# A mixing stage with half of its products on ScalarE and TensorE, the branch product first, and norms a tile earlier

## The reference, cut to what matters

```python
x_norm = x * rsqrt(mean(x * x) + RMS_EPS)
H_res_logits = x_norm @ W_res.T + H_res_base      # 4 x 4 per token
H_pre, H_post = softmax(...), softmax(...)        # 4 each per token
H_res = (1 - g) * I + g * sinkhorn_log(H_res_logits)
x_pre = einsum('btnc,btn->btc', x_streams, H_pre)
y = x_pre @ W_branch
x_mixed = einsum('btij,btjc->btic', H_res, x_streams)
return x_mixed + einsum('btc,btn->btnc', y, H_post)
```

## Time and profile before

| | us |
|---|---|
| median of three executions | 4292.85 |
| lowest and highest of them | 4287.7, 4294.64 |
| the profiled execution: its own time | 4291.77 |
| the profiled execution: its span | 4289.9 |
| logits block, 2537.9 to 2569.4 | 31.5 |
| mixing block, 2707.35 to 2785.5 | 78.15 |
| TensorE busy, whole span | 3957.4 (92%) |
| VectorE busy, whole span | 2181.7 (51%) |
| ScalarE busy, whole span | 1427.2 (33%) |

### The profile page before, as it was taken

How to read it: one execution, slowest core, us unless ns; L and a number is a source line. 1 busy time by engine, 2 the same in 40 slices (tenths; PEclk the granted TensorE clock), 3 DMA queues, 4 the chain that set the end, 5 groups by cost and what they waited for, 6 DMA issues and landing times. The chain is left out here.

```text
span 4289.9 us, 50949 instructions
## 1 busy us (share of the span) xinstructions
PE 3957.4 (92%) x18954; PEld 2122.3 (49%) x18954; DVE 2181.7 (51%) x3810; ACT 1427.2 (33%) x2586; POOL 313.2 (7%) x288
## 2 busy tenths in 40 slices
PE   8788989998988999999988779699999999999997
PEld 3333335554455555554446564355555445555554
DVE  0887755552247322224548418865655555444433
ACT  3777735552223211111113234311111133322232
POOL 1011002111001000000000111000000000000000
PEclk9999999999988999999998889999999999999998
DMA  4111121112001423211000121111001011111100
GB/s 184 44 40 36 60 68 38 35 35 72 30 28 50 161 101 108 99 35 70 0 27 1 40 100 34 46 41 40 20 20 40 1 66 35 35 35 40 55 15 23
DMA packets 133914, 215.09 MB, mean 50 GB/s; under 512 B 42704, under 2 KB 95056, under 8 KB 123072
## 3 DMA queue, kind: packets, MB, share of 16 engines
q1 hardware_dynamic: 133696, 212.06, 14.2%
HBM read 167.99 MB, written 44.04 MB: 49 GB/s over the span
## 5 line engine op out<-in xcount | busy, mean ns | idle before, releaser
L930 PE MATMUL l3a_po<-l3a_wo,l3a_cT 128*128 128x512 f32 x512 | 230.7, 604 | 3.1 <-ACT l3a_cT L1067 2.9
L436 PE MATMUL l1x_pj<-kvT,l1x_wq 128*128 128x512 f32 x512 | 228.3, 599 | 0.7 <-ACT kvT L240 0.7
L481 PE MATMUL l1x_po<-l1x_wo,l1x_cT 128*128 128x512 f32 x512 | 226.2, 596 | 1.2 <-issue 1.2
L819 PE MATMUL l3x_pj<-kvT,l3x_wq 128*128 128x512 f32 x512 | 225.5, 594 | 0.0
L819 PE MATMUL l3a_pj<-kvT,l3a_wq 128*128 128x512 f32 x512 | 224.9, 592 | 0.0
L577 DVE TENSOR_TENSOR x<-x,l1x_po 128x512 f32<-128x512 f32 x64 | 44.1, 689 | 266.9 <-PE l1x_po L481 266.9
L930 PEld LDWEIGHTS l3a_po<-l3a_wo,l3a_cT 128*128 128x128 f32 x512 | 95.6, 192 | 121.4 <-issue 110.9
L819 PEld LDWEIGHTS l3a_pj<-kvT,l3a_wq 128*128 128x128 f32 x512 | 95.5, 190 | 111.5 <-issue 111.4
L819 PEld LDWEIGHTS l3x_pj<-kvT,l3x_wq 128*128 128x128 f32 x512 | 95.5, 190 | 111.4 <-issue 111.4
L481 PEld LDWEIGHTS l1x_po<-l1x_wo,l1x_cT 128*128 128x128 f32 x512 | 95.7, 192 | 110.9 <-issue 110.9
L436 PEld LDWEIGHTS l1x_pj<-kvT,l1x_wq 128*128 128x128 f32 x512 | 94.6, 190 | 110.2 <-issue 107.2
(11 more groups left out here) (529 smaller groups left out, 7760.0 us busy)
## 6 DMA issues: line engine op xcount, KB each, us to landing
l1x_kb<-l1x_keys SPq DMA_DIRECT2D x32, 512.0 KB, 4.8
l1x_vb<-l1x_values SPq DMA_DIRECT2D x32, 512.0 KB, 3.4
l1x_keys<-l0a_kv SPq DMA_DIRECT2D x40, 256.0 KB, 2.0
fill_wk<-in_L_xattn_Wk SPq DMA_DIRECT2D x8, 1024.0 KB, 5.5
kvT<-in_L_xattn_Wv SPq DMA_DIRECT2D x8, 1024.0 KB, 5.8
l1x_values<-l0a_kv SPq DMA_DIRECT2D x32, 256.0 KB, 2.3
l1x_wq<-in_L_xattn_Wq SPq DMA_DIRECT2D x8, 1024.0 KB, 4.9
l1x_sbias<-in_L_xattn_bias SPq DMA_DIRECT2D x8, 1024.0 KB, 7.4
```

What stands on the lines that cost most here:

```text
L436: mm = pe.matmul(pj[:, j, :], wq[:, u, k, h * DH:(h + 1) * DH], m.kvT[:, k, 1, 512 * j:512 * (j + 1)], start=k == 0, stop=k == KC - 1)
L481: mm = pe.matmul(po[:, t % 2, :], cT[:, u, h, t * P:(t + 1) * P], wo[:, u, h, :], start=h == 0, stop=h == GH - 1)
L819: mm = pe.matmul(pj[:, j, :], wq[:, u, k, h * DH:(h + 1) * DH], m.kvT[:, k, 1, 512 * j:512 * (j + 1)], start=k == 0, stop=k == KC - 1)
L930: mm = pe.matmul(outs[t % 2][:, :], cT[:, h, t * P:(t + 1) * P], wo[:, u, h, :], start=h == 0, stop=h == GH - 1)
```

## The change

In the mixing block, VectorE now adds only streams 0 and 1 to `m.x`. ScalarE multiplies streams 2 and 3 by their weights, eight products of 128x128 into a new tile `us`; TensorE sums the two halves of `us` into a PSUM tile `pmix` (two buffers, one of them the old `psum`) by two products with the identity; VectorE adds `pmix` to `m.x` in one instruction of 128x512. The branch product `py` now stands ahead of the unit in TensorE's program. ScalarE makes `xs` of the next tile after the `preT` copy, and waits for `mixed` of the tile before last only. In the logits block, `norm` of the next tile stands ahead of the wait for the logits.

```diff
+        pmix = [psum, st.ps("pmix", [P, 512])]
+        us = st.sb("us", [P, 2, NS, CW])
...
                 def body(n, u):
                     if not last(n):
+                        f.norm(act, n + 1)
                         act.wait_ge(l_ready, n + 1)
-                        f.act(act, n + 1, 1 - u)
+                        f.copy(act, n + 1, 1 - u)
...
+                def streams(n):
+                    if n >= 2:
+                        act.wait_ge(mixed, n)
+                    nc.scalar.activation(xs[:, n % 2, :], m.x[:, n, :], ACT.Identity, bias=f.shift[:, n:n + 1],
+                                         scale=f.rstd[:, n:n + 1]).then_inc(xs_ready, 1)
+
+                def scaled(n):
+
+                    act.wait_ge(xs_ready, n + 2)
+                    act.wait_ge(mix_ready, n + 1)
+                    for j in range(2, NS):
+                        for i in range(NS):
+                            ins = nc.scalar.activation(us[:, j - 2, i, :], xs[:, n % 2, j * CW:(j + 1) * CW], ACT.Identity,
+                                                       scale=tm[:, n, i, j:j + 1])
+                    ins.then_inc(us_ready, 1)
+
+                streams(0)
                 for n in range(T):
-                    u = n % 2
-                    act.wait_ge(mixed, n if u else n + 1)
-                    nc.scalar.activation(xs[:, u, :], m.x[:, n, :], ACT.Identity, bias=f.shift[:, n:n + 1],
-                                         scale=f.rstd[:, n:n + 1]).then_inc(xs_ready, 1)
+                    scaled(n)
                     act.wait_ge(pre_turned, n + 2)
                     act.wait_ge(y_ready, n + 1)
                     nc.scalar.copy(preT[:, :], f.pt[:, 0:P]).then_inc(preT_ready, 1)
+                    if n + 1 < T:
+                        streams(n + 1)
                     if n >= 2:
                         norm(n - 2)
...
                     pe.transpose(f.pt[:, 0:P], pre[:, :], m.ident[:, :]).then_inc(pre_turned, 1)
-                    for q in later(n):
-                        unit(pe, q)
+                    pe.wait_ge(us_ready, n + 2)
+                    if n >= 2:
+                        pe.wait_ge(mixed, n)
+                    for j in range(2):
+                        mm = pe.matmul(pmix[n % 2][:, :], m.ident[:, :], us[:, j].rearrange("p i c -> p (i c)"), start=j == 0, stop=j == 1)
+                    mm.then_inc(mix_ready, 1)
                     pe.wait_ge(preT_ready, n + 2)
                     pe.wait_ge(mixed, n + 1)
                     pe.matmul(py[:, 0:CW], preT[:, :], wb[:, :], start=True, stop=True).then_inc(y_ready, 1)
+                    for q in later(n):
+                        unit(pe, q)
...
-                    for j in range(NS):
+                    for j in range(2):
                         dve.wait_ge(mix_link, chain.behind)
                         for i in range(NS):
                             nc.vector.scalar_tensor_tensor(res(i), stream(j), tm[:, n, i, j:j + 1], res(i),
                                                                        ALU.mult, ALU.add).then_inc(mix_link, chain.next())
                     if n:
                         moments(n - 1)
+                    dve.wait_ge(mix_ready, n + 2)
+                    dve.wait_ge(mix_link, chain.behind)
+                    nc.vector.tensor_tensor(m.x[:, n, :], pmix[n % 2][:, :], m.x[:, n, :], ALU.add).then_inc(mix_link, chain.next())
```

More of the change, by code:

```diff
@@ L2802, in stage_l2_ffn @@
         preT_ready, y_ready, mixed = st.sem("preT_ready"), st.sem("y_ready"), st.sem("mixed")
-        mix_link = st.sem("mix_link")
+        mix_link, us_ready, mix_ready = st.sem("mix_link"), st.sem("us_ready"), st.sem("mix_ready")
         UNITS3 = FOLD + CTX_K + CTX_V
@@ L3220, in body @@
                 def body(n, u):
-                    per = 3 + NS * (NS - 1) + NS
+                    per = 3 + NS + NS + 1
                     chain.at(per * n)
```

## The result

The changed kernel takes **4316.9 us** (median of 4, 4315.5 to 4317.9), the kernel before 4292.5 in the same comparison: a ratio of 1.0056, interval 1.0044 to 1.0068, so 24 us slower. The forecast was 4298, "no change", with 4305 as its upper end.

The account below looks back on a forecast made before the run. The prediction took a ScalarE-TensorE circle to pace the logits block and VectorE the mixing block. Head -7.0, mixing +0.5 and clock +11.9 gave +5.4 on 4292.85, so 4298 us, range 4284 to 4305.

Parts of the forecast that it names:

- Head, -7.0: Logits block: with the norm ahead of the wait, six tiles take 2.61 us each, 7.0 us less in all.
- VectorE at 6.4 a tile: Mixing block: VectorE's own work falls from 8.06 to 6.4 us a tile, without setting the pace.
- The new ring: Mixing block: ScalarE's and TensorE's steps wait on each other without overlap, 8.78 us a tile; block +0.5 at full clock.
- The clock, +11.9: Mixing block: TensorE's idle in each tile drops its clock; seven slow stretches of 1.7 us, 11.9 us more.
- ring at full clock: Rival, mixing block: no slow clock, or up to three slow stretches; 4286 to 4291 us, chance 0.17.
- the case to which the prediction gave 0.06: Mixing block: eight slow stretches and an activation step of 0.29 us, counted as slower, over 4301.4 us.
- VectorE keeps the pace: Rival, mixing block: eight tiles of 6.4 in place of 8.06 us, time 4269 us, chance 0.05.
- the activations do not overlap: Rival, mixing block: ScalarE's eight products take 3.00 us a tile, 6.7 us more, time 4305 us, chance 0.16.
- the clock rising in the head: Rival, logits block: TensorE's clock rises, transposes get shorter, 3 us less, time 4295 us, chance 0.10.
- The sum's silent term: Stages behind the mixing block: no change was counted there, 0 us.
- its signs of being wrong: Mixing block: the forecast is wrong if tiles are 6.5 us apart or the block's granted clock is above 0.95.

Follow-up runs that it names:

- the queue reordered: Changed kernel plus 48 idle VectorE increments, with ScalarE's eight products of the next tile moved ahead of the current tile's eviction and `kvT` copy: 4272.8 us.
- the fillers: Changed kernel plus 48 idle VectorE increments, with two idle TensorE products added ahead of each tile's identity products: 4292.4 us.

## Why the prediction was wrong

Point by point:

- **Head, -7.0: right.** -7.1 in the trace, -7.2 as a kernel of its own.
- **VectorE at 6.4 a tile: right, and unused.** With the queue reordered it is 6.50.
- **The new ring: right in its members and order, too short.** It was 8.78 a tile; at full clock 9.14 was measured. The step between two activations was put at 0.255 from the earlier trace rows; here it is 2.45 = 7 x 0.294 + 0.39, so 0.29 of the missing 0.36. The row differs in form, which I didn't weigh: it adds a bias from a PSUM source, these scale from SBUF. Here the Trainium skill ("ScalarE: Activation LUTs", section "What ACT_TABLE_LOAD costs") was right and the nearest row wrong: the step of 293 ns and the 2.44 us for eight, estimates worked out from its figures, agree with the 294 ns and 2.45 us of the trace. Over the seven intervals between tiles the missing 0.36 are 2.5 us.
- **The clock, +11.9 as seven stretches of 1.7: the sum of seven right, in part by luck, and the last stretch left out.** Against the 81.4 of the ring at full clock the block of 96.3 has 14.9 of slow clock. From the first identity products to the last are 75.5 us, with the fillers 63.4, so the seven stretches cost 12.1. But they were not alike: one cost 3.0 (the tile of 12.16 against 9.14, with the clock down for 6.8 us), the others 1.1 to 1.7. The eighth falls on tile 7, where nothing hides it, and takes the identity products (3.78, reckoned as 1.72) and the two units behind (8.06 where the filler run has 7.03): 3.1. With the 2.5 of the steps and some 0.7 that I haven't traced this is the block's missing 6.3. What the block did, eight stretches and a step of 0.29, is the case to which the prediction gave 0.06. Its rivals "ring at full clock" and "VectorE keeps the pace" fell, and so did "the activations do not overlap" (a step of 0.294, not 0.32 or more) and the clock rising in the head, where it stayed at 0.50.
- **The sum's silent term, nothing behind the block: the step that failed.** With +6.3 in the block alone the kernel would have come out at about 4304, inside the range. The rest is +12.0 in code that the change does not touch, and it alone would have carried the 4298 past its upper end. The sum had been built from the two blocks of the edits. It left the Sinkhorn block alone with a reason ("since nothing in it changes") and the stages behind with none, and none of its signs of being wrong looked there. Shown by the runs: the place of VectorE's following code decides it, in both directions, with an otherwise unchanged kernel. Argued, not shown: that the packets of q14 are the loads of VectorE's program, since a packet names no engine (they come and go with this program's length alone, and begin in the gaps behind its branches), and that the standstill of 2.9 us is the wait for them.

The 4272.8 us show what the change could have given: -7 for the head and -14 for the block, if ScalarE's products stand in its queue where the wait for the unit doesn't reach them.

## What to carry to other kernels

When work is handed to another engine, look for its place in that engine's queue before its duration: here the same eight activations of 2.45 us made the block 33 us longer behind the eviction than ahead of it, the slow clock included. A recurring wait on TensorE of the 2.8 to 2.95 us seen here costs twice, once itself and once in the clock of what follows, and idle products in it can pay for themselves. A change of code length shifts all code behind it; if stages change that the diff doesn't touch, compare the packets of the instruction queues and the waits at "issue", and repeat the comparison with idle instructions that restore the old place before judging the change.

## What the runs showed of the hardware

- 24 to 80 instructions more or less on VectorE moved the time of loops far behind by 12 to 13 us (0.3%), with q14 at 77 packets instead of 66 or 67, and 128 more brought the packets back to the old number. A standstill was 2.9 us and lay right behind the branch at the end of VectorE's loop.
- The clock's loss doesn't need a longer wait than that: with 2.78 or 2.95 us of idle in each tile 4 to 9 matmul instructions started at half clock in every tile, while with 1.23 the mean stayed at 0.97 over the block. The length of one idle doesn't decide it: of the two idles of 2.89 in layer 3 the first was followed by half clock and the second was not, nor was the one of 3.11 in the earlier trace rows. The Trainium skill ("TensorE: Matmul & The Clock Gate", section "A second HAM failure mode: psum-queue depth-cycling") reports short idles between groups of matmuls that let the clock swing between its two levels; the traces here agree for 2.8 us, not for 1.23.
- Adding 32 matmul instructions of 128x512 that compute nothing needed shortened a block by 13.4 us.
